# Selective-scan kernel: one VectorE scan per state over two PSUM banks, TensorE's order per state, and the place of the gate

## The reference

```python
x = x + gt_a * _attention(xm, Wqkv, Wproj, bproj)      # 16 heads, causal
x = x + gt_m * (gelu(xm @ W1 + b1) @ W2 + b2)
...
xs, z = split(h @ in_w);  xs = silu(xs);  proj = xs @ xproj_w
dt = softplus(proj[..., :512] + dt_bias);  B, C = proj's last 64 + 64;  A = -exp(A_log)
def step(hst, ins):
    dt_t, B_t, C_t, x_t = ins
    dA = jnp.exp(dt_t[:, :, None] * A)
    hst = hst * dA + (dt_t * x_t)[:, :, None] * B_t[:, None, :]
    y_t = jnp.einsum('bds,bs->bd', hst, C_t)
y = scan over the 256 times + xs * Dskip
return y * silu(z) @ out_w
...
x = x + gate * (h_fwd + h_bwd)                         # forward and flipped
x = x + gate * ((silu(h @ mlp_w1) * (h @ mlp_w2)) @ mlp_w3)
```

## Time and profile before

| | us |
|---|---|
| time of the runs, median of 3 | 3402.99 (3399.81 to 3408.39) |
| the profiled execution's own time | 3408.53 |
| its span, first to last instruction | 3406.7 |
| TensorE matmul busy | 3024.2 (89%) |
| ScalarE busy | 2989.0 (88%) |
| GpSimd busy | 2945.7 (86%) |
| VectorE busy | 2909.5 (85%) |
| mean granted clock of TensorE | 0.947 of full |

### The profile page before, as it was taken

How to read it: one execution, slowest core, us unless ns; L and a number is a source line. 1 busy time by engine, 2 the same in 40 slices (tenths; PEclk the granted TensorE clock), 3 DMA queues, 4 the chain that set the end, 5 groups by cost and what they waited for, 6 DMA issues and landing times.

```text
span 3406.7 us, 69419 instructions
## 1 busy us (share of the span) xinstructions
PE 3024.2 (89%) x21944; PEld 2683.9 (79%) x21944; DVE 2909.5 (85%) x3331; ACT 2989.0 (88%) x6469; POOL 2945.7 (86%) x1552
## 2 busy tenths in 40 slices
PE   8778898999988999899988999899998899998776
PEld 6568787888878888788877888788887888887765
DVE  3269998899888998889988999889988899899885
ACT  1189999899989999899999999899998999999994
POOL 0069998999888998889988998889988899899995
PEclk6689999999989999899999999899998999999998
DMA  4011111111111111111111111112111111111210
GB/s 174 0 42 43 48 45 47 42 51 48 43 48 47 47 47 42 49 45 48 45 47 43 49 48 43 48 41 52 48 43 46 48 47 46 42 45 45 54 47 26
DMA packets 163033, 162.50 MB, mean 48 GB/s; under 512 B 17610, under 2 KB 156874, under 8 KB 162644
## 3 DMA queue, kind: packets, MB, share of 16 engines
q1 hardware_dynamic: 162644, 157.69, 17.2%
HBM read 154.44 MB, written 3.18 MB: 46 GB/s over the span
## 4 chain that ended last, share of the span: by engine, by line
PE 45%; POOL 16%; ACT 15%; issue 13%; DVE 9%; DMA 1%; DVEq 1%; POOLq 0%; ACTq 0%; SPq 0%
POOL hst L408 12%; PE ps L1225 12%; PE ps L1241 11%; ACT dA L567 7%; PE ps L993 6%; ACT uBT L553 4%; DVE hst L892 4%; PE ps L1002 4%; POOL uBT L417 4%; PE ps L1065 3%; PE ps L1040 2%; PE ps L1114 1%; PE ps L1049 1%; PE ps L1233 1%; PE ps L1150 1%
## 5 line engine op out<-in xcount | busy, mean ns | idle before, releaser
L408 POOL TENSOR_TENSOR hst<-hst,C_sb 128x1024 f32<-128x1024 f32 x1024 | 2441.0, 2409 | 232.8 <-DVE hst L892 226.6
L892 DVE TENSOR_TENSOR_SCAN hst<-dA,ps 128x512 f32<-128x512 f32 x2048 | 2384.0, 1205 | 177.6 <-PE ps L1241 160.1
L567 ACT ACTIVATE dA<-dt,A 128x255 f32<-128x255 f32 x4096 | 1758.5, 504 | 2.8 <-DVE hst L892 2.7
L1225 PE MATMUL ps<-ident,uBT 128*128 128x128 f32 x8192 | 1288.2, 281 | 134.0 <-DVE hst L892 103.0
L1241 PE MATMUL ps<-ident,hst 128*128 128x128 f32 x8192 | 1267.9, 278 | 104.5 <-POOL hst L408 103.7
L1225 PEld LDWEIGHTS ps<-ident,uBT 128*128 128x128 f32 x8192 | 994.2, 145 | 299.0 <-DVE hst L892 152.5
L553 ACT ACTIVATE uBT<-uT,BT 128x512 f32<-128x512 f32 x1536 | 1052.2, 720 | 130.9 <-PE ps L1225 120.0
L1241 PEld LDWEIGHTS ps<-ident,hst 128*128 128x128 f32 x8192 | 979.6, 144 | 139.8 <-POOL hst L408 139.7
L417 POOL TENSOR_TENSOR uBT<-uT,BT 128x512 f32<-128x512 f32 x512 | 559.3, 1092 | 185.3 <-DVE uT L829 185.3
L476 ACT ACTIVATE probs<-ps,nmax 128x128 f32<-128x128 f32 (+1 forms) x256 | 93.9, 423 | 101.6 <-DVE nmax L764 100.7
L993 PE MATMUL ps<-xsT,w_xp 128*128 128x256 f32 x512 | 130.6, 380 | 0.0
(11 more groups left out here) (142 smaller groups left out, 2110.7 us busy)
## 6 DMA issues: line engine op xcount, KB each, us to landing
C_sb<-c_dram SPq DMA_DIRECT2D x1024, 128.0 KB, 2.9
gate_l<-gate_rows_dram SPq DMA_DIRECT2D x16, 256.0 KB, 3.7
x_att<-in_x_dram SPq DMA_DIRECT2D x8, 256.0 KB, 3.0
w<-in_L_cond_W_dram SPq DMA_DIRECT2D x2, 1024.0 KB
out_dram<-x_glu SPq DMA_DIRECT2D x8, 256.0 KB, 3.2
wg<-in_L_cond_mlp_w_dram SPq DMA_DIRECT2D x3, 512.0 KB, 11.4
w_xp<-_L_cond_fwd_xproj_w_dram SPq DMA_DIRECT2D x1, 1280.0 KB, 12.4
w_xp<-_L_cond_bwd_xproj_w_dram SPq DMA_DIRECT2D x1, 1280.0 KB, 15.0
```

The source lines that it names most:

```text
L408: pool.tensor_tensor(h, h, C_sb[:, n % FED:n % FED + 1, :].to_broadcast([P, KI, NB]), ALU.mult).then_inc(hC_ready.sem, 1)
L567: done = act.activation(dA[:, n % NT, c, lo:hi], dt[:, d, c, lo:hi], ACT.Exp, scale=A[:, d, c, n:n + 1])
L892: dve.tensor_tensor_scan(pair(hst[:, n % NR]), pair(dA[:, n % NT]), ps[:, BANK_U + (2 * n + e) % (2 * NU), :][:, way], 0.0, ALU.mult, ALU. ...
L1225: last = pe.transpose(ps[:, BANK_U + (2 * n + e) % (2 * NU), o:o + P], uBT[:, n % NF, j, c * P:(c + 1) * P], ident[:, :])
```

## The change

On VectorE a state is scanned by one instruction over two PSUM banks (1024 columns), at n.1; nothing but the steps is left at n.0. So the order on VectorE is: steps of n.0, scan n, steps of n.1. On TensorE place n.0 has the whole `sum_state(n-3)` and then its steps, and n.1 the whole `force(n+1)` and its steps; the force used to stand first and now follows the sum. `gate_y` stands before scan 2 instead of inside scan 3. `uB_ready`, `scan_done` and `y_mm` count whole states; the wait of ScalarE's decays for a scan is made once a state. Plan, tiles, arithmetic and the number of transposes are the same.

```diff
-        uBT_ready, uBT_pooled, uB_ready, dA_ready = flow("uBT_ready"), flow("uBT_pooled", NS // 2), flow("uB_ready", 2), flow("dA_ready", 2)
-        scan_done, hC_ready, y_mm = flow("scan_done", 2, 2 * NT), flow("hC_ready", 1, FED), flow("y_mm", 2, 2 * NR)
+        uBT_ready, uBT_pooled, uB_ready, dA_ready = flow("uBT_ready"), flow("uBT_pooled", NS // 2), flow("uB_ready"), flow("dA_ready", 2)
+        scan_done, hC_ready, y_mm = flow("scan_done", 1, NT), flow("hC_ready", 1, FED), flow("y_mm", 1, NR)
...
-                if r_known(p, n) >= NT:
-                    act.wait_ge(scan_done.sem, scan_done.at(p * NS + n, (2 if n < NT else e + 1) - 2 * NT))
+                if e == 0 and r_known(p, n) >= NT:
+                    act.wait_ge(scan_done.sem, scan_done.at(p * NS + n, 1 - NT))
...
                 def state(n, e):
 
+                    if e == 0:
+                        return
                     r = p * NS + n
-                    if n == BEHIND and e == 1 and not very_first:
+                    if n == BEHIND - 1 and not very_first:
                         gate_y(p - 1, 1 - d)
-                    dve.wait_ge(y_mm.sem, y_mm.at(r, e + 1 - 2 * NR))
-                    dve.wait_ge(dA_ready.sem, dA_ready.at(r, e + 1))
-                    dve.wait_ge(uB_ready.sem, uB_ready.at(r, e + 1))
-                    pair = lambda t: t[:, 2 * e:2 * e + 2, :].rearrange("p k n -> p (k n)")[:, way]
-                    dve.tensor_tensor_scan(pair(hst[:, n % NR]), pair(dA[:, n % NT]),
-                                           ps[:, BANK_U + (2 * n + e) % (2 * NU), :][:, way], 0.0, ALU.mult, ALU.add).then_inc(scan_done.sem, 1)
+                    dve.wait_ge(y_mm.sem, y_mm.at(r, 1 - NR))
+                    dve.wait_ge(dA_ready.sem, dA_ready.at(r, 2))
+                    dve.wait_ge(uB_ready.sem, uB_ready.at(r, 1))
+                    bank = BANK_U + 2 * n % (2 * NU)
+                    line = lambda t: t.rearrange("p k n -> p (k n)")[:, way]
+                    dve.tensor_tensor_scan(line(hst[:, n % NR]), line(dA[:, n % NT]), line(ps[:, bank:bank + 2, :]),
+                                           0.0, ALU.mult, ALU.add).then_inc(scan_done.sem, 1)
...
-            def force(p, n, e):
+            def force(p, n):
...
-                    pe.wait_ge(scan_done.sem, scan_done.at(r, e + 1 - 2 * NU))
-                for c in range(2 * e, 2 * e + 2):
+                    pe.wait_ge(scan_done.sem, scan_done.at(r, 1 - NU))
+                for c in range(KI):
...
-                    if n + 1 < NS:
-                        force(p, n + 1, e)
-                    elif not very_last:
-                        force(p + 1, 0, e)
-                    if n == BEHIND and e == 0:
+                    if e == 1:
+                        if n + 1 < NS:
+                            force(p, n + 1)
+                        elif not very_last:
+                            force(p + 1, 0)
+                        return
+                    if n == BEHIND:
                         start_y(p, d)
                     if n >= BEHIND:
-                        sum_state(p * NS + n - BEHIND, n - BEHIND, e)
+                        sum_state(p * NS + n - BEHIND, n - BEHIND)
                     elif not very_first:
-                        sum_state(p * NS + n - BEHIND, NS + n - BEHIND, e)
+                        sum_state(p * NS + n - BEHIND, NS + n - BEHIND)
```

More of the change, by code:

```diff
@@ L1234, in start_y, with sum_state @@
                                   start=(c == 0), stop=False, skip_group_check=True)
[L1236 to L1239 removed]
+            def sum_state(r, n):
+                pe.wait_ge(hC_ready.sem, hC_ready.at(r, 1))
+                for c in range(KI):
                     for j in range(TT):
@@ L1314, in _ @@
             pe.wait_ge(late_in, N_LATE)
-            for e in range(2):
-                force(0, 0, e)
+            force(0, 0)
             period(0, False, True)
@@ L1321, in _ @@
             for n in range(NS - BEHIND, NS):
-                for e in range(2):
-                    sum_state((2 * NBLK - 1) * NS + n, n, e)
+                sum_state((2 * NBLK - 1) * NS + n, n)
             for _ in post(NBLK - 1, 1):
```

21 lines of the change are left out of this document (8 added, 13 removed).

## The result

The change makes the kernel slower: 3422.5 us (median of 6 runs, 3418.0 to 3433.5) beside 3406.1 us for the kernel before in the same runs, ratio 1.0056, 95% interval 1.0037 to 1.0075. The profiled execution took 3417.97 us (span 3416.2) at a granted clock of 0.951, where that of before had 0.947. So the forecast of 3371 was wrong by 51 us and on the wrong side, and the range ended at 3412.

The account below looks back on a forecast made before the run. The limit was taken to change hands among TensorE, GpSimd with ScalarE, and VectorE. Gains of 4.1 us a period over seven periods, 29 us, plus 3 from the heads made 32: from the median 3402.99 to 3371 us, range 3335 to 3412.

Parts of the forecast that it names:

- (c): End of the backward pass: TensorE's 2.48 us wait for dt times x shrinks by 1.1 us a period.
- (b): Norms: ScalarE gets statistics earlier; 1.5 and 1.0 us for two norms, 0.9 in the forward pass, 3.4 us a period.
- (a): Gate at the start of a forward pass: TensorE's 1.36 us stop shrinks to 0.3 to 0.4, gaining 1.0 us a period.
- (d): Given back: 1.0 us a period entering the forward heads behind scan 40, 0.4 for forces completed later.
- (e): Stall in the forward softplus: TensorE's 3.70 us stop becomes about 4.8; counted zero, 1.1 either way, 8 us in all.
- One scan for two: VectorE's scan of 1024 columns takes 2.26 us; gains 3 us in all, in the backward heads.
- The 154 us of busy time: VectorE's scans: one at 2.26 us for 2 x 1.205 was to save about 154 us of busy time.
- The slower one: Rival: TensorE held behind whole scans, a period 3.5 us longer, +24, 3427 us; chance 0.20.
- GpSimd's rival: GpSimd keeps the time, so only a few us of the norms' gain last: 3398 us; chance 0.15.
- The clock's: Rival: one more half-clock stretch of TensorE a period, +35 us, 3406 us; chance 0.03.

Follow-up runs that it names:

- one-input steps: Four softplus steps of VectorE read one SBUF tensor, part of the computation left out: kernel before 3375.1 us (0.9907), changed kernel 3371.6 us (0.9903).
- gate alone: Kernel before with only the gate product moved, from between the halves of scan 3 to ahead of them: 3393.9 us, 0.9966.
- halves back to back: Changed kernel with two half scans back to back in the place of each whole scan: 3432.7 us, ratio 1.0080 to the kernel before.

## Why the prediction was wrong

The sum was 4.1 us gained in each period; the loop's bodies lost 1.5. Term by term:

**(c), the end of the backward pass, is the step that failed.** It reasoned that dt times x "stood behind the first half of scan 58 and will stand before it: 1.1 us". It does stand before it, and the transposes that wait for it came 1.9 us later, counted from the start of the last projection (38.4 us where it was 36.5). With one-input steps, without the collisions, the same stretch takes 34.6 us in the kernel before and 33.7 in the changed one: then the 1.1 us is there, or nearly. The half scan that used to stand between L822 and L826 had let L826 meet only the end of GpSimd's product by C (2.25 us); now it comes when that product has just begun and lasts 3.26, and L815 and L818 ahead of it last 1.9 us longer together. The sum had no term for an instruction's duration depending on its neighbour, although the trace of before held 1.95 beside 1.23 us for L815 and 2.25 beside 1.19 for L822 and L826, and the diff puts pairs of them together. With the collisions away the two kernels are level (0.9903 and 0.9907): so they account for the loss, and not for the whole of the gain that is missing. That needs two more steps of the prediction.

**What was never counted: the entry to the backward heads.** 2.4 us a period lost. The sum had no term for it, and I had written that TensorE reaches the force half a state later, when the scan is more often done. For 1.1 of the 2.4 us it is not. The prediction also had ScalarE's waits "order nothing new", since the decays lead the scans by two states. They wait 64.2 us for scans where it was 2.7. All of ScalarE's idle time is the same (418.7 us of the span, 417.7 before), so that this cost anything is not shown.

**(b), the norms: right in kind, too large.** ScalarE's waits for the statistics in the rows that answer to the earlier trace rows:

```profile
1278.53 0.30 ACT L448 ACTIVATE rstd<-mv,eps_col 128x2 f32<-128x2 f32 x1 [1.97 <-DVE mv L703]
1318.81 0.29 ACT L448 ACTIVATE rstd<-mv,eps_col 128x2 f32<-128x2 f32 x1 [0.33 <-DVE mv L703]
```

0.93 and 1.18 us shorter than 2.90 and 1.51, "shorter by about 1.1" as promised. But TensorE gained 0.8 over the first norm and 0.3 over the second, not 1.5 and 1.0. Over the norm of the forward pass, for which 0.9 was counted, it lost 0.3; there ScalarE had no wait for statistics in the kernel before. So (b) came to 0.8 us a period and not 3.4. Why TensorE gets less than ScalarE's shorter waits was not followed.

**(a), the gate: right and too small.** 1.0 us a period was the idle time of one gate less what stays. By itself the early gate brings 2.5 us a period and 0.34%, 12 us (gate alone); taking it back in the changed kernel costs 0.24%, with intervals that overlap. For the backward pass the prediction took nothing, and that was wrong on the face of the trace of before: TensorE's wait there, 1.12 us at 1193.87, is nearly that of the earlier trace rows. Here is the gate after; "under 0.5" before the skip products was 0.54:

```profile
997.48 1.23 DVE L878 TENSOR_TENSOR gT<-ps,sz 128x1024 f32<-128x1024 f32 x1 [1.40 <-PE ps L1242]
998.76 1.49 PE L1235 MATMUL ps<-skip_diag,xsT 128*128 128x128 f32 x11 [0.54 <-DVE gT L878]
```

**(d), what is given back,** and **(e), the softplus of the forward pass.** The stall of the earlier trace rows grew from 3.70 to 4.58 us ahead of the force at 1064.29, close to the 4.8 named, but (e) then counted zero; and L822 behind it takes 3.27 us where it took 2.25. At 0.8 us lost in this stretch (14.7 us between two sets of transposes, 13.9 before) (e) lay within its own bounds, and the cause was again the collision and not the stop: with one-input steps the stretch takes 12.6 us in the changed kernel and 12.8 in the one before. (d) was not measured apart.

**One scan for two.** 2.26 us forecast, 2278 ns measured; 3 us in all forecast, about 8 measured against halves back to back, with intervals that overlap. The 154 us of busy time was misread: the halves overlap, 2048 of them make 2384.0 us of busy time and not 2048 x 1.205 = 2468, so only 67 us of it went. The 128 us that the prediction worked out from the Trainium skill, "VectorE: DVE Perf Modes", section on the TRN2 errata, were far off as well: of 2 x 1205 - 2278 = 132 ns saved in each state, 135 us in all, little reaches the time.

**The rivals.** The slower one forecast 3427 and had the sign and nearly the size, which is luck. Its mechanism, TensorE held behind the whole scan, is there (force waits 154.0 us against 103.0), and at the entry it decides 1.1 us; yet with the collisions gone the changed kernel isn't slower than before. GpSimd's rival was right that GpSimd didn't wait less (230.6 us, 226.6 before). The clock's can be excluded: 0.951 granted, 0.947 before, and 150 us at half clock in the six loop bodies where it was 164. In the product stretches and in the forward heads the limits stayed as in the earlier trace rows (windows of the same places: PE, PEld, DVE, ACT, POOL busy, clock, DMA):

```profile
998.80:1058.40 59.60, 59.39 (x442) 53.12 (x443) 51.15 (x35) 55.64 (x119) 54.28 (x29) 1.00 0.18 44
1145.00:1156.00 11.00, 10.64 (x90) 9.54 (x89) 10.79 (x13) 11.00 (x27) 11.00 (x7) 1.00 0.19 46
```

## What to carry to other kernels

Where one kind of instruction shows several durations in a trace (1.19 and 2.25 us for one form), find out what it met before moving anything near it; merging two instructions also removes the gap between their neighbours. Cost a merge by the order it leaves: the saved 132 ns a state bought some 8 us, and the order of TensorE that goes with it cost 38 when it was tried alone. And try the smallest part of a change alone: the gate, moved by one half scan, brought 12 us where the sum had 7 for it, and is faster than both kernels.

## What the runs showed of the hardware

VectorE and GpSimd exclude each other for whole instructions where a VectorE instruction reads two tensors from SBUF and GpSimd's reads SBUF. In the loop's bodies 1.19 us becomes up to 3.27 on VectorE, 2.37 becomes 3.26 (L408) and 1.05 becomes 2.03 (L417) on GpSimd; one L815 behind the loop took 5.25. Neither one-input VectorE steps (1.19 to 1.22 us in the same places) nor scans with one input in PSUM (2.25 to 2.29 us inside GpSimd's instructions) are held. Sixty-four such steps of VectorE cost the kernel before 0.9% of its time and the changed one 1.5%. A scan over two banks took 2278 ns, over one 1205: by these two, as an estimate, 2.1 ns a column and about 0.13 us fixed.
